# Engine choice tile by tile and a new head in an 8-bit feed-forward kernel with per-sample mixing

## The reference

```python
y   = einsum('bct,bcd->bdt', x, weights[token]).reshape(-1, 512).astype(bfloat16)
quant(v, inv): v = v * inv; s = max(max|v| / 127, 1e-8); return round(v / s), s
qg, sg = quant(y, inv_gate);  qu, su = quant(y, inv_up)
gate = (qg @ w_gate.T) * sg * s_wgate        # 512 -> 256
up   = (qu @ w_up.T)   * su * s_wup
m    = clip(silu(gate) * up, -10, 10).astype(bfloat16)
qi, si = quant(m, inv_inter)
out  = x + (qi @ w_down.T) * si * s_wdown    # 256 -> 512
```

## Time and profile before

| what | value |
|---|---|
| median of 3 runs | 91.86 us (91.46 to 93.71) |
| the profiled execution | 91.56 us, its span 89.8 us |
| last DVE operation ends | about 87.3 us; then the last store |
| busy in the span | DVE 70.5, ACT 67.0, PE 64.8, POOL 63.8 us |

### The profile page before, as it was taken

The page is one execution under the profiler, slowest core; times in us unless marked ns, Lnnn a source line. Parts: engine busy times, 40 slices in busy tenths (PEclk is TensorE's granted clock), DMA queues, the critical chain, the costliest instruction groups (busy, mean ns, idle before and its releaser), DMA issues.

```text
span 89.8 us, 1762 instructions
## 1 busy us (share of the span) xinstructions
PE 64.8 (72%) x481; PEld 40.4 (45%) x481; DVE 70.5 (79%) x155; ACT 67.0 (75%) x123; POOL 63.8 (71%) x55
## 2 busy tenths in 40 slices
PE   5929999867944996958676869598767739894620
PEld 5914668564613544724343546163525425581100
DVE  3013955959899698899999899999999897989760
ACT  5022268998998799994999999799999996717300
POOL 2001949580399479799997979999988499994550
PEclk9999999999999999999999999999999995699855
DMA  2799944927026860581061061253030004345036
GB/s 28 211 335 379 341 150 106 361 75 237 3 36 82 329 221 7 131 297 39 0 183 51 4 180 54 102 139 117 0 117 0 0 7 170 149 152 200 37 133 225
DMA packets 9341, 12.09 MB, mean 135 GB/s; under 512 B 3314, under 2 KB 4210, under 8 KB 9330
## 3 DMA queue, kind: packets, MB, share of 16 engines
q1 hardware_dynamic: 8640, 11.63, 40.1%
q0 software_dynamic: 80, 0.26, 1.0%
q10 hardware_dynamic: 610, 0.07, 0.5%
HBM read 7.50 MB, written 4.46 MB: 133 GB/s over the span
## 4 chain that ended last, share of the span: by engine, by line
DVE 24%; PE 24%; issue 15%; ACT 14%; POOL 13%; DMA 5%; ACTq 0%; DVEq 0%; POOLq 0%
POOL xs L251 10%; PE gu_ps L716 6%; PE y_ps L684 6%; ACT q_t L325 6%; DMA table<-in_L_cond_weights 5%; DVE ffn L520 5%; DVE gu L476 5%; DVE y_ps L459 4%; PE qmt_ps L639 4%; DVE y_ps L504 2%; ACT q L318 2%; DVE clipped L488 2%; POOL res L267 2%; POOL xm L260 2%; DVE gu_ps L481 2%
## 5 line engine op out<-in xcount | busy, mean ns | idle before, releaser
L251 POOL TENSOR_TENSOR xs<-y_bf,inv_in 128x1024 f32<-128x1024 bf16 x15 | 32.1, 2142 | 6.2 <-ACT y_bf L301 6.2
L716 PE MATMUL gu_ps<-w_t,q_t 128*128 128x256 bf16 x128 | 16.9, 279 | 6.7 <-ACT q_t L325 5.6
L684 PE MATMUL y_ps<-x_sb,mix_all 128*128 128x512 f32 x30 | 18.1, 688 | 4.7 <-ACT mix_all L352 1.8
L267 POOL TENSOR_TENSOR res<-ffn,x_sb 128x512 f32<-128x512 f32 x15 | 18.9, 1270 | 2.8 <-DVE ffn L520 2.8
L318 ACT ACTIVATE q<-xs,rscale 128x512 f32<-128x512 f32 x30 | 19.9, 716 | 0.2 <-DVE rscale L470 0.2
L459 DVE TENSOR_REDUCE y_ps<-xs 128x2 f32<-128x1024 f32 x14 | 17.1, 1220 | 0.4 <-POOL xs L251 0.2
L716 PEld LDWEIGHTS gu_ps<-w_t,q_t 128*128 128x128 bf16 x128 | 11.8, 99 | 12.0 <-ACT q_t L325 7.9
L325 ACT ACTIVATE q_t<-qt_ps 128x1024 bf16<-128x1024 f16 x15 | 15.1, 1021 | 0.3
L260 POOL TENSOR_TENSOR xm<-clipped,inv_mid 128x256 f32<-128x256 bf16 x15 | 10.1, 675 | 5.8 <-DVE clipped L488 4.8
L476 DVE TENSOR_TENSOR gu<-gu_ps,s_in 128x512 f32<-128x512 f32 x16 | 11.0, 685 | 3.4 <-PE gu_ps L716 3.4
L301 ACT ACTIVATE y_bf<-y_ps 128x512 bf16<-128x512 f32 x15 | 8.9, 591 | 4.3 <-PE y_ps L684 4.2
(11 more groups left out here) (60 smaller groups left out, 64.7 us busy)
## 6 DMA issues: line engine op xcount, KB each, us to landing
x_sb<-in_x SPq DMA_DIRECT2D x16, 256.0 KB, 3.4
out<-res SPq DMA_DIRECT2D x16, 256.0 KB, 2.0
raw<-in_L_ffn_w_gate SPq DMA_DIRECT2D x1, 512.0 KB, 6.0
raw<-in_L_ffn_w_up SPq DMA_DIRECT2D x1, 512.0 KB, 4.9
raw<-in_L_ffn_w_down SPq DMA_DIRECT2D x1, 512.0 KB, 5.1
inv_in<-in_L_ffn_inv_gate SPq DMA_DIRECT2D x1, 256.0 KB, 4.4
inv_in<-in_L_ffn_inv_up SPq DMA_DIRECT2D x1, 256.0 KB, 4.9
s_out<-in_L_ffn_s_wdown SPq DMA_DIRECT2D x1, 256.0 KB, 5.4
```

The costliest lines, as they stand in the source:

```text
L251: nc.gpsimd.tensor_tensor(xs[t % 3][:, :, :], y_bf[t % 3][:, :].unsqueeze(1).to_broadcast([P, 2, T]), inv_in[:, :, :], ALU.mult).then_inc( ...
L267: nc.gpsimd.tensor_tensor(res[t % RES][:, :], ffn[t % 3][:, :], x_sb[:, t * T:(t + 1) * T], ALU.add).then_inc(res_done, 1)
L684: nc.tensor.matmul(y_bank(t)[:, :], mix_all[:, t, :], x_sb[:, t * T:(t + 1) * T], start=True, stop=True).then_inc(y_done, 1)
L716: last = nc.tensor.matmul(gu_ps[p][:, m, :], q_t[p][:, m, c, :], w_t[j][:, m, c * I:(c + 1) * I], start=(j == 0 and c == 0), stop=(j == pa ...
```

## The change

Five strings of one letter per tile choose the engine (V for DVE, P for POOL, A for ACT) of the clip, the middle smoothing, its quantisation, its eviction and the residual. 15 of 16 clips move from DVE to POOL; 6 more middle smoothings move to DVE (tiles 0, 2, 4, 6, 8, 10; tile 15 was there); 6 middle quantisations move from ACT to POOL; 3 evictions move from ACT to DVE; of the residuals tiles 2 and 12 move to DVE. Since POOL cannot read PSUM, the product that it clips goes to a new SBUF tile `inter`. The middle's scale and reciprocal become instructions of their own for all tiles, and the reciprocals are separate entries in the list.

At the head the table's load is the first DMA, issued by SP; the table serves tiles 0, 1 and 2 (DVE and ACT), single-block DMAs only tile 3, and the gather tiles 4 to 15. The large memset of `mix_all` moves from DVE to POOL, one weight eviction from DVE to ACT, and the three `rest_in` to ACT's tail. The loads of x no longer wait for earlier tiles. All engines' lists are in a new order.

```diff
-    EARLY = 6
+    EARLY = 4
     WARM_UP, WARM_DRAIN = 36, 20
     RES = 4
-    AHEAD = 5
-    LAG = 3
+
+    CLIP_ON, MID_ON, QM_ON = "PPPPPPPPPPPPPPPV", "VPVPVPVPVPVPPPPV", "PPPPAPAAAPAAAAAA"
+    QM_OUT_ON, RES_ON = "VAAVAAAAAAAAAAAV", "PPVPPPPPPPPPVPPV"
+
+    def nth(table, t):
+        return table[:t + 1].count(table[t])
 
     x_rows = x.rearrange("b c t -> (b c) t")
...
+            sp.dma_start(table[:, :, :], mix_w.rearrange("s c d -> c s d")).then_inc(table_in, 16)
             load(0)
             broadcast(inv_gate, inv_in[:, 0, :], inv_gate_in)
             broadcast(inv_up, inv_in[:, 1, :], inv_up_in)
             load(1)
             load_weight(0, w_gate)
-            sp.wait_ge(row_in, 16)
-            sp.wait_ge(mix_zero, 1)
-            picked_blocks(2, PER // 2)
             load(2)
             load_weight(1, w_up)
             load(3)
             broadcast(s_gate, s_in[:, 0, :], scales_in)
             broadcast(s_up, s_in[:, 1, :], scales_in)
-            picked_blocks(3, 0)
+            sp.wait_ge(row_in, 16)
+            sp.wait_ge(mix_rest_zero, 1)
+            picked_blocks(3)
             broadcast(inv_inter, inv_mid[:, :], mid_in)
             load_weight(2, w_down)
-            broadcast(s_down, s_out[:, :], s_out_in)
             load(4)
-            sp.wait_ge(mix_zero, 2)
-            picked_blocks(4, 0)
-            load(5)
             sp.wait_ge(picked_in, 16)
             sp.dma_start(picked_dram, picked[:, :]).then_inc(picked_out, 16)
-            picked_blocks(5, 0)
+            broadcast(s_down, s_out[:, :], s_out_in)
+            load(5)
             sp.wait_ge(picked_out, 16)
             for j in range(PER):
                 sp.dma_start(mix_all[j * C:(j + 1) * C, EARLY:TILES, j * C:(j + 1) * C],
                              picked_dram.rearrange("(k j) (c d) -> j c k d", j=PER, c=C)[j, :, EARLY:TILES, :]
                              ).then_inc(blocks_in, 16)
-            for t in range(6, 11):
+            for t in range(6, TILES):
...
+            def clip(t):
+                pool.wait_ge(inter_done, t + 1)
+                if t >= 2:
+                    pool.wait_ge(xm_done[MID_ON[t - 2]], nth(MID_ON, t - 2))
+                nc.gpsimd.tensor_scalar(clipped[t % 2][:, :], inter_of(t), LIMIT, -LIMIT,
+                                        ALU.min, ALU.max).then_inc(clip_done["P"], 1)
+
             def smooth_mid(t):
-                if t == 0:
-                    pool.wait_ge(mid_in, 16)
-                pool.wait_ge(clip_done, t + 1)
-                if t >= 2:
-                    pool.wait_ge(qm_done, t - 1)
+                pool.wait_ge(mid_in, 16)
+                pool.wait_ge(clip_done[CLIP_ON[t]], nth(CLIP_ON, t))
+                if t >= 2:
+                    pool.wait_ge(qm_done[QM_ON[t - 2]], nth(QM_ON, t - 2))
                 nc.gpsimd.tensor_tensor(xm[t % 2][:, :], clipped[t % 2][:, :], inv_mid[:, :],
-                                        ALU.mult).then_inc(xm_done, 1)
+                                        ALU.mult).then_inc(xm_done["P"], 1)
+
+            def quantise_mid(t):
+                pool.wait_ge(rscalem_done, t + 1)
+                if t >= 2:
+                    pool.wait_ge(qmt_done, t - 1)
+                nc.gpsimd.tensor_scalar(qm[t % 2][:, :], xm[t % 2][:, :], rscale_m[:, t:t + 1], ROUND_TO_F16,
+                                        ALU.mult, ALU.add).then_inc(qm_done["P"], 1)
...
+            pool.memset(mix_all[:, 3:TILES, :], 0.0).then_inc(mix_rest_zero, 1)
...
+            smooth_second_half(); smooth(1); smooth(2); smooth(3); smooth(4)
+            smooth(5); clip(0); smooth(6); clip(1); quantise_mid(0)
+            smooth_mid(1); smooth(7); smooth(8); quantise_mid(1); clip(2)
+            clip(3); smooth_mid(3); smooth(9); smooth(10); clip(4)
+            clip(5); quantise_mid(2); quantise_mid(3); smooth_mid(5); smooth(11)
+            smooth(12); clip(6); clip(7); quantise_mid(5); smooth_mid(7)
+            residual(0); smooth(13); clip(8); clip(9); residual(1)
+            smooth(14); smooth_mid(9); smooth(15); residual(3); residual(4)
+            clip(10); clip(11); quantise_mid(9); smooth_mid(11); residual(5)
+            residual(6); clip(12); clip(13); smooth_mid(12); smooth_mid(13)
+            residual(7); residual(8); clip(14); smooth_mid(14); residual(9)
+            residual(10); residual(11); residual(13); residual(14)
...
+            def weight_out(m):
+                act.wait_ge(wt_done, m + 1)
+                nc.scalar.activation(w_t[0][:, m, :], wt_ps[m], ACT.Copy).then_inc(wt_out[m], 1)
...
+            weight_out(1); q_out_second_half(); y_out(3); quantise(1); y_out(4)
+            q_out(1); quantise(2); y_out(5); gate_silu(0); quantise(3)
+            gate_silu(1); y_out(6); q_out(2); q_out(3); quantise(4)
+            y_out(7); quantise(5); gate_silu(2); y_out(8); q_out(4)
...
+            rest_in(0); gate_silu(15); qm_out(11); quantise_mid(12); quantise_mid(13)
+            qm_out(12); rest_in(1); qm_out(13); quantise_mid(14); quantise_mid(15)
+            qm_out(14); rest_in(2)
...
-                n = 3 if t >= LAG else 2
                 dve.wait_ge(amax_done, t + 1)
-                if t >= LAG:
-                    dve.wait_ge(amaxm_done, t - LAG + 1)
-                nc.vector.tensor_scalar(scale[:, t, 0:n], y_bank(t)[:, 0:n], 1.0 / QMAX, LEAST_SCALE,
+                nc.vector.tensor_scalar(scale[:, t, :], y_bank(t)[:, 0:2], 1.0 / QMAX, LEAST_SCALE,
                                         ALU.mult, ALU.max).then_inc(scale_done, 1)
+
+            def reciprocal_in(t):
                 dve.wait_ge(scale_done, t + 1)
-                nc.vector.reciprocal(rscale[:, t, 0:n], scale[:, t, 0:n]).then_inc(rscale_done, 1)
...
+                nc.vector.scalar_tensor_tensor(inter_of(t), gu[t % 2][:, 1, :], scale[:, t, 1:2],
...
+            def smooth_mid(t):
+                dve.wait_ge(mid_in, 16)
+                dve.wait_ge(clip_done[CLIP_ON[t]], nth(CLIP_ON, t))
+                if t >= 2:
+                    dve.wait_ge(qm_done[QM_ON[t - 2]], nth(QM_ON, t - 2))
+                nc.vector.tensor_tensor(xm[t % 2][:, :], clipped[t % 2][:, :], inv_mid[:, :],
+                                        ALU.mult).then_inc(xm_done["V"], 1)
+
+            def qm_out(t):
+                dve.wait_ge(qmt_done, t + 1)
+                if t >= 2:
+                    dve.wait_ge(down_done, t - 1)
+                nc.vector.tensor_scalar(qm_t[t % 2][:, :, :], qmt_ps[:, t % 2, 0:IC, :], -float(OFFSET), None,
...
+                nc.vector.tensor_tensor(res[t % RES][:, :], ffn[t % 3][:, :], x_sb[:, t * T:(t + 1) * T],
+                                        ALU.add).then_inc(res_done["V"], 1)
...
-            dve.memset(mix_all[:, 4:TILES, :], 0.0).then_inc(mix_zero, 1)
...
+            smooth_first_half(); amax_half(0); amax_half(1); scale_half(0); reciprocal_half(0)
+            scale_half(1); reciprocal_half(1); q_out_first_half(); amax_in(1); scale_in(1)
+            reciprocal_in(1); weight_out(0); amax_in(2); amax_in(3); scale_in(2)
+            reciprocal_in(2); scale_in(3); reciprocal_in(3); gate_up_out(0); amax_in(4)
+            scale_in(4); gate_up_out(1); intermediate(0); weight_out(2); amax_in(5)
+            smooth_mid(0); scale_in(5); reciprocal_in(4); amax_mid(0); intermediate(1)
...
+            down_out(11); smooth_mid(15); amax_mid(14); amax_mid(15); scale_mid(14)
+            reciprocal_mid(14); scale_mid(15); down_out(12); reciprocal_mid(15); residual(12)
+            down_out(13); qm_out(15); down_out(14); down_out(15); residual(15)
...
+            mix_in_batch(0); keep_warm(2, free_in_head); mix_in_batch(1); weight(0); mix_in_batch(2)
+            transpose_q_half(0); weight(1); transpose_q_half(1); mix_in_batch(3); keep_warm(34, free_in_head)
+            mix_in_batch(4); transpose_q(1); gate_up(0); mix_in_batch(5); weight(2)
```

306 lines of the change are left out of this document (127 added, 179 removed).

## The result

The changed kernel takes 96.25 us (median of 4 runs, 95.53 to 98.15), beside 92.78 us for the kernel before on the same chip (4 runs, 91.46 to 93.84): ratio 1.047, 95% interval 1.035 to 1.060. It is slower, outside the forecast's range. The profiled execution took 96.12 us with a span of 94.3 us, against 91.56 and 89.8. Ratios leave out runs that a slower state of the chip disturbed (where too few were left for one, none is given), and the traces of e2, e4 to e9, e14, e17 and e18 are of such slower runs.

The account below looks back on a forecast made before the run. From 20 to 75 us DVE and ACT, 92% and 93% busy, were taken as the bound, with a waiting head and a drain through DVE. Sum: 91.56 + 0 (head) - 1.3 (DVE's work) - 2.0 (idle) + 1.5 (port) = 89.8 us; range 86.3 to 94.4.

Parts of the forecast that it names:

- the forecast's range: Whole kernel's time: 86.3 to 94.4 us around a forecast of 89.8 us.
- I take 0: Head: first gate/up eviction at 19 to 22 us against 19.85 before, cost taken as 0 (bounds -1 and +2).
- a mark on DVE: DVE's first gate/up eviction, from which the prediction counted DVE's work and idle; forecast at 19 to 22 us.
- tile 4's blocks land after 20 us: Head: a sign that would show the forecast wrong; the blocks were forecast to land at 17 to 19 us.
- late-head rival: Head: tile 4's blocks land at 19, first eviction at 21.9, middle gains nothing; 92.3 us, chance 0.20.
- The port: +1.5 forecast: Middle: DVE's six smoothings and two residuals with two SBUF inputs wait for POOL; +1.5 us (bounds 0 and +5.2).
- The upper bound, 5.2: Port term: eight DVE operations each wait POOL's mean rest of 0.65 us, 5.2 us in all.
- one row in which only half the overlap was lost: DVE's row at 9.79 beside POOL's half smoothing from 10.11, which lost 0.16 of 0.31 us.
- DVE's work: -1.3 forecast: DVE behind the first eviction: 8.5 us off, 7.2 on; net -1.3 us (bounds -3.8 and +0.2).
- the bound of -3.8: DVE's work behind the first eviction: the lower bound of its net change, 3.8 us less.
- Idle: -2.0 forecast: DVE's idle in middle and drain, 6.6 us before: -2.0 us (bounds 0 and -4.4).
- packed rival: Middle and drain: DVE's idle falls by its bound of 4.4 us, port costs 0.5; 86.4 us, chance 0.17.

Follow-up runs that it names:

- e2: Changed kernel with the six moved middle smoothings and residuals 2 and 12 back on POOL: 98.3 us, no ratio given.
- e4: Changed kernel with spill first, the six smoothings and two residuals back on POOL, and tile 4 later in the lists: 98.23 us, 1.067.
- e9: e1 with groups of 11 unused PE products in the head's gaps: 93.66 us, ratio 1.015.
- e14: e1 with tiles 4 and 5 straight from the matrices, inv_inter and w_down loaded before tile 5's blocks, and unused PE products: 98.91 us, ratio 1.069.
- e17: Kernel before with only the changed kernel's front (table first, early gather, tiles 4 to 15 by spill and read-back), old lists and places: 91.96 us, ratio 0.991.
- e18: Kernel before with the head of e15, without its unused products: 95.0 us, ratio 1.033.
- e3: Changed kernel with tile 4's work behind tiles 0 and 1 on PE, ACT and DVE, and clips 0 and 1 ahead on POOL: 95.13 us, 1.034.
- e10: e1 with tiles 4 and 5 taken straight from the matrices, their blocks ahead of the spill: 100.73 us, ratio 1.099.
- e11: e1 with six clips moved to DVE, these and tile 15's writing to PSUM: 105.12 us, ratio 1.146.
- e6: Kernel before with six middle smoothings moved to DVE, clipped value of these and tile 15 in PSUM: 94.3 us, no ratio given.
- e5: Same as e6 in every instruction, but with the clipped value in SBUF: 102.35 us, ratio 1.104.
- e1: Changed kernel with SP's list alone changed: spill ahead of the loads of inv_mid, w_down, s_out and x 5: 94.6 us, ratio 1.021.
- e15: e1 with only tile 4 straight from the matrices, w_down's load ahead of its blocks, and unused PE products: 93.45 us, ratio 1.014.
- e7: e1 with tiles 0 and 1's products, evictions and intermediates ahead of tile 4's work on PE, ACT and DVE: 95.34 us, ratio 1.038.
- e8: e7 with residuals 2 and 12 back on POOL: 96.27 us, ratio 1.041.
- e12: e11 joined with e10 and e9: 111.62 us, ratio 1.218.
- e16: e15 with the list order of e7: 94.88 us, ratio 1.030.

## Why the prediction was wrong

**The step that failed: "I take 0" for the head.** As a mark on DVE it was wrong by 7.6 us (19 to 22 forecast, 27.49 measured). The terms of its chain were taken from a trace in which gather and spill had gone out later, at 8.97 and 19.75, among other neighbours on the queues: the gather landed at 12.9 and not 9 to 11, the spill took 6.0 and not 3.2, and the read-backs began at 18.86. The prediction itself named "tile 4's blocks land after 20 us" as what would refute it, and its late-head rival (21.9, 92.3 us) had the mechanism with about a quarter of the size (2.0 of 7.6). What neither saw is that this mark has no fixed price. e3 put it at 20.9 with the time hardly changed, e10 at 21.1 with the time longer by 4.5, and e17 has the same transfers and loses nothing. The lateness arises from the chain together with the new lists, which hang tiles 0 and 1 on tile 4; what it costs in time the mark does not say.

**The sum was cut at a mark that other runs don't keep.** With the new lists and places of work the tail was 58.7 to 61.6 us in all kernels but the two with e11's edit; with the old ones 54.5 to 55.2 (56.0 with e6's edit, 64.5 with e5's waits at the port), wherever tile 6 came. So from this mark on the new lists and places take some 4 to 6 us more than the old ones, and e17 shows from the other side that the new front's transfers cost nothing by themselves. A better head only made up for part of it (e1, e15). This does not clear the new order of the head, since part of what stands behind the mark is DVE work that the old lists do ahead of it; e3 and e7, which brought 2.1 us of it forward (15.97 and 15.94 us done at the mark), had tails shorter by only 0.7 and 0.9 us. Nor is it the granted clock: over the tail it was 0.91 in the changed kernel and 0.95 in the one before, but e2, with 0.94, has a tail of 60.6 us.

**The port: +1.5 forecast for eight operations, +4.4 measured for them, +5.8 with tile 15's two.** The upper bound, 5.2, had the rest of POOL's running instruction as the price of every such operation, and the sum came near it. The order helped three of the six smoothings; they cost 0.34 us each (0.15 forecast), but the two residuals 1.2 each (0.3 forecast). I had taken the term down on the order and on one row in which only half the overlap was lost; there POOL waited for DVE's short operation, and that row says nothing of DVE behind a smoothing of 2.14. The pair e5 and e6 shows that it is the second SBUF input: 1.276 against 0.418 us. The Trainium skill, page "SBUF — State Buffer", section "SBUF: two separate sides", states that whichever of the two starts first holds the shared ports for its whole instruction; the prediction cited this and did not follow it. The traces agree, with DVE as the one that waits (32.38 and 63.31 us) and at 42.53 us with POOL, whose smoothing took 0.95 us in place of 0.67 beside DVE's of 0.42. With the term at +5.2 the sum would have been an estimated 93.5, still 2.6 short of the profiled execution.

**DVE's work: -1.3 forecast, about -4.6 measured** (busy +1.2, less the 5.8), just past the bound of -3.8. The durations of DVE's rows behind the first eviction add up to 66.9 us before and 72.5 after, so without the 5.8 they changed by -0.2 (the forecast's terms give +0.3 with the small operations at full price). The rest is that the rows lie over one another by 10.5 us in place of 6.1: 4.3 more, where the forecast allowed 1.6. **Idle: -2.0 forecast, -4.5 measured**: that is the packed rival's amount. POOL's clip took 0.40 (0.45 estimated), its quantisation 0.49, tile 0's mixing came at 4.88 (5.4). DVE was packed as that rival said, but with the port's waiting in the packing, and behind a first eviction 7.6 us late.

**Why the port is not the whole of the 4.7.** Giving all eight operations back to POOL left the tail as it was (e2): POOL then has 57.4 us of 60.6. With only the residuals given back (e8), 1.5 us of waiting are left where e7 has 4.5, and the tail is 0.3 us shorter than e7's; POOL has 55.1 us of 58.7. Both engines are near full after the change (DVE 57.9 and POOL 53.0 of 59.9 us), and a middle smoothing costs 0.865 us on DVE and 0.775 on POOL, so moving it bought nothing on either. What was not run is the changed kernel without the waits and with all else as it is: e11 tried it and put another wait in their place. On the old lists the same waits did cost time (e5 against e6). How the 4.7 us divide between the port, the 6.5 us of DVE work left over at 32 us, and the new order stays open: the old lists with the new places of work, or the reverse, was not run.

## What to carry to other kernels

- Before an operation is moved from POOL to DVE, count its SBUF inputs. With two, its price here was its own length and, where POOL had started first, the rest of what POOL had in flight; with one in PSUM it was its own length (0.418 us). Ask also what holding PSUM for it keeps waiting.
- A tile whose blocks come late by a chain of small DMAs cost nothing where no in-order list had earlier tiles' work behind it (e17). Read that from the lists, not from the transfer times; and where a load is moved back on a queue, name its reader, which is the next wait.
- Cut the account where the full stretch begins, and try the cut on a second kernel before it is believed: one half of the change under the other half's old version (e17) showed here in one run what fourteen variants of the changed kernel had not: that the new transfers were not the loss.

## What the runs showed of the hardware

- An indirect gather on POOL's queue took 5.0 to 5.3 us where it was issued at 8.7 to 9.3 us (before, e5, e6), and 7.6 to 9.1 issued at 4.3 to 4.6 among the first large loads. The 256 KB spill took 2.9 to 4.0 where w_down was not just ahead of it on the queue (4.3 in e18), and 5.6 to 6.1 behind w_down and x 4.
- DVE's product of 256 columns took 0.41 to 0.42 us with one input in PSUM (e6), and 0.42 to 2.10 with both in SBUF beside POOL's work (e5). The waiting shows as the length of DVE's row, not as idle time ahead of it.
- POOL with one input over 256 columns: 0.399 us for clip to bfloat16, 0.487 for the quantisation to float32; its memset of 1664 float32 columns took 1.484 us.
- PE's mixing took 1.08 us at the higher granted clock (16.57 us in the changed kernel) and 2.04 to 2.08 at the lower (13.09 and 23.32). The granted clock does not tell all: the kernel before has mixings of 2.05 and 2.02 us at 6.86 and 9.87, where its profile shows 1.00. In the changed kernel the clock was at the lower level (1.2 GHz) from 9.4 to 16.5 us, behind a wait of PE of 1.91 us for x 1 and through waits of 1.22 for w_gate and 1.08 for x 2. The five kernels with the unused products put in there (e9, e12, e14, e15, e16) had it at the higher level (2.4 GHz) for the first 20 us; the ten others with the new lists all had a lower stretch ahead of 17 us.
